# A routing that chooses on logits, gates that are a softmax over two, and slots read from the banks

## The reference

```python
logits = jnp.einsum('bsd,de->bse', x, gate_w) + gate_b
probs = jax.nn.softmax(logits, axis=-1)
top_probs, top_idx = jax.lax.top_k(probs, 2)
top_probs = top_probs / jnp.sum(top_probs, axis=-1, keepdims=True)
dispatch = jnp.sum(jax.nn.one_hot(top_idx, n_experts, dtype=x.dtype) * top_probs[..., None], axis=-2)
h1 = jnp.einsum('bsd,edh->bseh', x, w1)
h2 = jnp.einsum('bsd,edh->bseh', x, w2)
hidden = jax.nn.silu(h1) * h2
expert_out = jnp.einsum('bseh,eho->bseo', hidden, w3)
return jnp.einsum('bseo,bse->bso', expert_out, dispatch)
```

## Time and profile before

| | |
|---|---|
| median of 3 runs | 683.85 us (684.36, 678.06, 683.85) |
| the profiled execution | 683.36 us, span 681.3 us |
| mean granted clock of TensorE | 0.905 of 2.4 GHz |
| TensorE busy | 554.9 us, 81% |
| VectorE busy | 348.6 us, 51% |
| GpSimd busy | 408.2 us, 60% |
| ScalarE busy | 342.1 us, 50% |

### The profile page before, as it was taken

One profiled execution on the slowest core, in us unless ns is written; L12 is line 12 of the kernel. 1 busy time (PEld: TensorE's weight loads), 2 busy tenths in 40 slices (PEclk: granted clock), 3 DMA queues, 4 the chain that ended last, 5 costly groups with the idle time before them and its releaser, 6 DMA issues.

```text
span 681.3 us, 15719 instructions
## 1 busy us (share of the span) xinstructions
PE 554.9 (81%) x5422; PEld 468.6 (69%) x5423; DVE 348.6 (51%) x1021; ACT 342.1 (50%) x801; POOL 408.2 (60%) x468
## 2 busy tenths in 40 slices
PE   2477788778779999999999999959649729999960
PEld 2466667657547777677777678748639729999960
DVE  6977787846620171212001274784875405555563
ACT  4467668886547243674122552522515406666640
POOL 1568789767567388675333330037747777777771
PEclk9689999979869699999999988978978959999995
DMA  8452322212055455322219200001123123333457
GB/s 296 161 140 82 85 73 81 67 47 70 13 180 201 154 174 171 128 94 99 88 47 331 61 1 1 0 23 52 52 61 98 52 85 99 98 97 98 128 204 242
DMA packets 56288, 72.15 MB, mean 106 GB/s; under 512 B 9086, under 2 KB 46934, under 8 KB 55614
## 3 DMA queue, kind: packets, MB, share of 16 engines
q1 hardware_dynamic: 49374, 58.36, 27.5%
q0 software_dynamic: 5120, 10.57, 4.7%
q10 hardware_dynamic: 1728, 2.36, 0.9%
HBM read 55.83 MB, written 21.69 MB: 114 GB/s over the span
## 4 chain that ended last, share of the span: by engine, by line
PE 56%; DVE 14%; POOL 9%; issue 9%; ACT 7%; DMA 3%; SPq 1%; POOLq 0%; DVEq 0%; ACTq 0%
PE bank L836 12%; PE bank L798 9%; PE bank L781 8%; PE bank L902 7%; PE bank L847 6%; POOL gathered_or_att L580 3%; POOL padded_or_w L571 3%; ACT normed L947 2%; POOL gathered_or_att L589 2%; PE bank L325 2%; DVE ln_stats L1133 2%; PE bank L796 2%; PE bank L827 2%; PE bank L733 2%; PE bank L867 1%
## 5 line engine op out<-in xcount | busy, mean ns | idle before, releaser
L615 POOL TENSOR_TENSOR padded_or_w<-padded_or_w,gathered_or_att 128x384 f32<-128x384 f32 x96 | 95.4, 1000 | 80.7 <-ACT padded_or_w L1021 77.0
L632 POOL DMA_INDIRECT sorted_x<-normed,slot x72 | 71.2, 989 | 80.0 <-DVE slot L1395 51.4
L1021 ACT ACTIVATE padded_or_w<-bank,moe_b 128x384 f32<-128x384 f32 x96 | 55.3, 579 | 107.2 <-PE bank L781 107.1
L651 POOL DMA_INDIRECT returned<-gathered_or_att,home_of_slot x88 | 87.2, 991 | 26.8 <-issue 19.8
L798 PEld LDWEIGHTS bank<-moe_or_conv,padded_or_w 128*128 128x128 f32 x576 | 80.6, 197 | 30.9 <-issue 9.8
L798 PE MATMUL bank<-moe_or_conv,padded_or_w 128*128 128x128 f32 x576 | 83.9, 284 | 0.0
L781 PE MATMUL bank<-chan_major,moe_or_conv 128*128 128x384 f32 x192 | 82.7, 517 | 0.1
L671 PE MATMUL bank<-padded_or_w 64*64 64x64 f32 x1152 | 47.5, 233 | 27.3 <-issue 15.9
L1459 DVE TENSOR_TENSOR att_or_moe<-att_or_moe,bank 128x256 f32<-128x256 f32 x88 | 37.0, 420 | 61.2 <-ACT att_or_moe L1035 39.9
L671 PEld LDWEIGHTS bank<-padded_or_w 64*64 64x64 f32 x1152 | 41.5, 145 | 36.6 <-issue 32.8
L580 POOL TENSOR_TENSOR gathered_or_att<-gathered_or_att,score_max 128x384 f32<-128x384 f32 x48 | 39.9, 830 | 34.5 <-DVE score_max L1217 33.7
(11 more groups left out here) (214 smaller groups left out, 1122.8 us busy)
## 6 DMA issues: line engine op xcount, KB each, us to landing
gathered_or_att<-combine SPq DMA_DIRECT2D x24, 768.0 KB, 4.2
padded_or_w<-windows SPq DMA_DIRECT2D x192, 48.0 KB, 2.0
sorted_x<-in_pad_rows SPq DMA_DIRECT2D x22, 260.0 KB, 7.1
padded_or_w<-sorted_x SPq DMA_DIRECT2D x22, 260.0 KB
padded_or_w<-in_moe_w SPq DMA_DIRECT2D x8, 512.0 KB, 5.4
qy<-returned SPq DMA_DIRECT2D x6, 384.0 KB, 5.8
out<-residual ACTq DMA_DIRECT2D x12, 192.0 KB, 2.1
normed<-returned SPq DMA_DIRECT2D x6, 384.0 KB, 5.4
```

The costliest lines, as they stand in the source:

```text
L615: nc.gpsimd.tensor_tensor(HB[n % DRING], HB[n % DRING], GB_[k % 3][:, n % 4, :], ALU.mult).then_inc(S("gated"), 1)
L632: nc.gpsimd.indirect_dma_start(xs_dram, bass.IndirectOffsetOnAxis(ap=POS[b][:, k, t:t + 1], axis=0), TNR[b][:, t, :], None).then_inc(S(don ...
L651: nc.gpsimd.indirect_dma_start(yt_dram, bass.IndirectOffsetOnAxis(ap=HOMES[b][:, j:j + 1], axis=0), YR[k * RING + j % RING], None).then_in ...
L1021: nc.scalar.activation(HB[n % DRING], banks[HBANK[n % 2]][:, 0:DG], ACT.Gelu, bias=B1C[:, e:e + 1]).then_inc(S("gelu"), 1)
```

## The change

The second routing (16 experts) takes its two experts by the largest logits instead of the largest probabilities, so that shift, exponential, sum and division fall away ahead of the choice. The gate is made of the two chosen logits: e = exp(second - first), first gate 1 / (1 + e), second e / (1 + e). VectorE signals the difference (`logit_gap`) right after the second maximum, ScalarE answers with an exponential of 18 values a partition (`gap_exp`). In the list, `RE` moves to the middle of ScalarE's six normalization groups, and `RC` piece 0 behind them; VectorE has no part in those groups, so its own order is the same. A chosen logit is taken out by adding -1e38 where a probability was by adding -2.

In the slots, the matrix of ones meets the mask read in expert order, so that the counts lie in bank 7 as the scan wants them, and the scan reads the bank. The 0/1 factors that restart the scan at each expert (SAME) and the matrix TRO = TRI - ONE are built once, in `centre_gate`. As TRO's product subtracts the tokens from this one to its tile's end, the sum that includes the tile can be used as it is, and the subtraction of the tile's count goes. The two products change places.

```diff
@@ -175,6 +175,9 @@
         LGP = [sb(f"logits_of_norm{b}", [P, TT * EX[1]]) for b in range(NB)]
+        GEXP = sb("gate_exp", [P, TT])
+        SAME = sb("same_expert", [P, EX[1] * TT])
+        TRO = sb("not_before", [P, P])
         GST = sb("gn_stats", [P, 6, 6])
...
@@ -807,8 +810,8 @@
                 pe.wait_ge(S("chosen"), b + 1)
-                nc.tensor.matmul(banks[6][:, 0:TT * E], TRI, RT[:, 5, 0:TT * E], start=True, stop=True)
-                nc.tensor.matmul(banks[7][:, 0:TT * E], ONE, RT[:, 5, 0:TT * E], start=True, stop=True).then_inc(S("prefix"), 1)
+                nc.tensor.matmul(banks[7][:, 0:TT * E], ONE, RT[:, 5, 0:TT * E].rearrange("p (t e) -> p e t", e=E), start=True, stop=True)
+                nc.tensor.matmul(banks[6][:, 0:TT * E], TRO[:, :], RT[:, 5, 0:TT * E], start=True, stop=True).then_inc(S("prefix"), 1)
@@ -1008,9 +1011,10 @@
                     t_wait_read(act, group_no[("LG", l, b)])
+                    nc.scalar.activation(RT[:, 1, 0:TT * EX[l]], RT[:, 0, 0:TT * EX[l]], ACT.Exp).then_inc(S("logit_exp"), 1)
                 else:
-                    act.wait_ge(S("logit_shift"), b + 1)
-                nc.scalar.activation(RT[:, 1, 0:TT * EX[l]], RT[:, 0, 0:TT * EX[l]], ACT.Exp).then_inc(S("logit_exp"), 1)
+                    act.wait_ge(S("logit_gap"), b + 1)
+                    nc.scalar.activation(GEXP[:, :], RV[:, 3, :], ACT.Exp).then_inc(S("gap_exp"), 1)
@@ -1260,8 +1264,6 @@
                         link(tt(row(0), row(0), over_t(GB[:, :]), ALU.add))
-                        link(nc.vector.tensor_reduce(v[0], row(0), AX, ALU.max))
-                        tt(row(0), row(0), over_e(v[0]), ALU.subtract).then_inc(S("logit_shift"), 1)
                         return
@@ -1269,7 +1271,7 @@
-                if piece == 1:
+                if piece == 1 and l == 0:
                     dve.wait_ge(S("logit_exp"), n + 1)
@@ -1277,19 +1279,24 @@
                     k = piece - 2
-                    link(nc.vector.tensor_reduce(v[k], row(1), AX, ALU.max))
-                    link(tt(row(0), row(1), over_e(v[k]), ALU.is_equal))
-                    link(tt(row(0), row(0), over_t(REV[:, 0:E]), ALU.mult))
-                    link(nc.vector.tensor_reduce(v[2], row(0), AX, ALU.max))
-                    link(tt(row(2 + k), row(0), over_e(v[2]), ALU.is_equal))
+                    a, same, out_of = (row(1), row(0), -2.0) if l == 0 else (row(0), row(1), -1e38)
+                    link(nc.vector.tensor_reduce(v[k], a, AX, ALU.max))
+                    if l and k:
+                        tt(v[3], v[1], v[0], ALU.subtract).then_inc(S("logit_gap"), 1)
+                    link(tt(same, a, over_e(v[k]), ALU.is_equal))
+                    link(tt(same, same, over_t(REV[:, 0:E]), ALU.mult))
+                    link(nc.vector.tensor_reduce(v[2], same, AX, ALU.max))
+                    link(tt(row(2 + k), same, over_e(v[2]), ALU.is_equal))
                     if k == 0:
-                        link(nc.vector.scalar_tensor_tensor(row(1), row(2), -2.0, row(1), ALU.mult, ALU.add))
+                        link(nc.vector.scalar_tensor_tensor(a, row(2), out_of, a, ALU.mult, ALU.add))
...
                         tt(row(5), row(2), row(3), ALU.add).then_inc(S("chosen"), 1)
-                    link(tt(v[2], v[0], v[1], ALU.add))
-                    if l == 0:
+                        dve.wait_ge(S("gap_exp"), b + 1)
+                        link(ts(v[2], GEXP[:, :], 1.0, None, ALU.add))
+                    else:
+                        link(tt(v[2], v[0], v[1], ALU.add))
                         link(nc.vector.tensor_scalar_max(v[2], v[2], 1e-12))
@@ -1297,8 +1304,8 @@
                         dve.wait_ge(S("homes_set"), 2 * NB)
-                        tt(TNR[b][:, :, P + 1], v[0], v[3], ALU.mult)
-                        tt(NEXT[b][:, :, 1], v[1], v[3], ALU.mult).then_inc(S("first_gates"), 1)
+                        nc.vector.tensor_copy(TNR[b][:, :, P + 1], v[3])
+                        tt(NEXT[b][:, :, 1], GEXP[:, :], v[3], ALU.mult).then_inc(S("first_gates"), 1)
@@ -1308,6 +1315,9 @@
                 m = group_no[("GC", k)]
+                link(nc.vector.memset(SAME[:, :], 1.0))
+                link(nc.vector.memset(SAME[:, :].rearrange("p (e t) -> p e t", t=TT)[:, :, 0:1], 0.0))
+                link(tt(TRO[:, :], TRI, ONE, ALU.subtract))
                 t_wait_full(dve, m)
@@ -1353,19 +1363,12 @@
                 dve.wait_ge(S("prefix"), b + 1)
-                tot = RT[:, 0, 0:c].rearrange("p (e t) -> p e t", t=TT)
-                one = RT[:, 1, 0:c].rearrange("p (e t) -> p e t", t=TT)
-                nc.vector.memset(RT[:, 1, 0:c], 1.0).then_inc(S("dve_chain"), 1)
-                chain[0] += 1
-                link(nc.vector.tensor_copy(tot, banks[7][:, 0:c].rearrange("p (t e) -> p e t", e=E)))
-                link(nc.vector.memset(one[:, :, 0:1], 0.0))
-                link(nc.vector.tensor_tensor_scan(RT[:, 4, 0:c], RT[:, 1, 0:c], RT[:, 0, 0:c], 0.0, ALU.mult, ALU.add))
+                link(nc.vector.tensor_tensor_scan(RT[:, 4, 0:c], SAME[:, :], banks[7][:, 0:c], 0.0, ALU.mult, ALU.add))
                 run_ = RT[:, 4, 0:c].rearrange("p (e t) -> p e t", t=TT)
...
                 tmp = RT[:, 1, 0:c].rearrange("p (e t) -> p e t", t=TT)
-                nc.vector.tensor_copy(cnt, run_[:, :, TT - 1])
-                link(tt(tot, run_, tot, ALU.subtract))
+                link(nc.vector.tensor_copy(cnt, run_[:, :, TT - 1]))
@@ -1384,10 +1387,10 @@
-                link(tt(row(4), tot.rearrange("p e t -> p t e"), banks[6][:, 0:c].rearrange("p (t e) -> p t e", e=E), ALU.add))
-                link(tt(row(1), row(4), over_t(room), ALU.is_ge))
+                link(tt(row(0), run_.rearrange("p e t -> p t e"), banks[6][:, 0:c].rearrange("p (t e) -> p t e", e=E), ALU.add))
+                link(tt(row(1), row(0), over_t(room), ALU.is_ge))
                 link(tt(row(1), row(1), over_t(delta), ALU.mult))
-                link(tt(row(4), row(4), over_t(base), ALU.add))
+                link(tt(row(4), row(0), over_t(base), ALU.add))
                 link(tt(row(4), row(4), row(1), ALU.add))
...
                     link(tt(row(0), row(2 + k), row(4), ALU.mult))
```

More of the change, by code:

```diff
@@ L248, in metaformer_program @@
                   *taps(1, 0, 9), *[(kind, 0, g) for g in range(NG) for kind in ("XZ", "LZ")], *groups("AN", "XL", 1), *taps(1, 9, 15),
-                  *normed("LR", 1, 0)[:3], ("RC", 1, 0, 0), ("RE", 1, 0), *groups("LT", "LR", 1, 0), *choice(1, 0, 1, 6), *taps(1, 15, 42), ("RP", 0), *taps(1, 42, 54),
+                  *normed("LR", 1, 0)[:3], *groups("LT", "LR", 1, 0)[:3], ("RE", 1, 0), *groups("LT", "LR", 1, 0)[3:], ("RC", 1, 0, 0), *choice(1, 0, 1, 6), *taps(1, 15, 42), ("RP", 0), *taps(1, 42, 54),
                   ("RS", 0), ("GN", "XM", 1), ("KW", 6, "hc_ready", 2 * NB), ("GS", "XM", 1), ("GQ", "XM", 1), ("XMH", 1), ("RJ", 0),
                   *[("XU", 1, n) for n in range(8)], ("GN", "XU", 1), ("KW", 30, "up_out", 8 * NB), ("GS", "XU", 1), ("GQ", "XU", 1), ("KW", 10, "up_out", 8 * NB), *groups("XUH", 1), *[(kind, 1, g) for g in range(NG) for kind in ("XZ", "LZ")],
-                  *normed("LR", 1, 1)[:3], ("RC", 1, 1, 0), ("RE", 1, 1), *groups("LT", "LR", 1, 1), ("KW", 34, "up_out", 8 * NB), *choice(1, 1, 1, 6), ("RP", 1), ("KW", 16, "up_out", 8 * NB), ("RS", 1), ("RJ", 1),
+                  *normed("LR", 1, 1)[:3], *groups("LT", "LR", 1, 1)[:3], ("RE", 1, 1), *groups("LT", "LR", 1, 1)[3:], ("RC", 1, 1, 0), ("KW", 34, "up_out", 8 * NB), *choice(1, 1, 1, 6), ("RP", 1), ("KW", 16, "up_out", 8 * NB), ("RS", 1), ("RJ", 1),
                   *[("M", b) for b in range(NB)], *[("F", b) for b in range(NB)]]
```

## The result

| | before | changed |
|---|---|---|
| median | 684.01 us (20 runs, 678.06 to 689.9) | 680.28 us (20 runs, 673.05 to 686.64) |
| ratio | | 0.993, 95% interval 0.9901 to 0.9958 |
| profiled execution | 683.36 us, span 681.3 | 681.42 us, span 679.4 |

Some executions of either kernel run at a lower granted clock and take over 1.5% longer than its fastest; the ratio leaves them out, the medians don't. The change is worth 0.7%, 4.8 us, with an interval of 2.9 to 6.8 us. That interval holds the forecast gain of 6.24 us as well, so the time alone can't say which of the prediction's terms came true; the traces can.

A forecast was written before the change was run, and what follows sets the result against it. The path was taken to run through VectorE's routing chain in image 1, and its slots in both images, to the scatter. 2.57 + 2.36 + 1.31 = 6.24 us gain, forecast 677.5 us, range 672.5 to 681.5.

The forecast's parts named there:

- rival A: Image 1's products: TensorE's clock has fallen when the mask comes; gain 4.93 us, 678.9 by the median; chance 0.20.
- B: Ones product's stepped mask read costs 0.5 us in each image; gain 5.24, or 3.9 with rival A; chance 0.10.
- Part 5: Matrix-of-ones product reading the mask in steps of 16 values: taken at 0, upper bound 0.5 us an image.
- Part 7: Image 1's two products: TensorE's clock taken as still high, a gain of 1.31 us; lower bound 0.
- Part 1: No softmax ahead of the second routing's choice: gain 2.57 us in image 1; image 0's 2.6 gained and lost again.
- Part 2: Gates from an 18-element exponential after nine of ScalarE's normalizations: covered, two us of slack, put at nothing.
- Parts 3 and 4: Slots from the banks: gain 1.18 us an image; scan reading a bank: 0, bounds 0 to 0.19 an image.
- Part 6: Two fills and a subtraction built once ahead of VectorE's gate centring: nothing, 0.7 us without the idle time there.
- C: Clock stays high under image 1's second convolution and first fillers: 3.2 us more, 674.4; chance 0.10.
- D: Image 0's 1.18 us from the slots are lost because something other than VectorE is late there: 678.8; chance 0.06.
- E: Scatter or send-back follows a pace of its own, so nothing arrives: 683.9; chance 0.05.
- F: Stepped mask read many times dearer than doubled, a loss from 2.5 us an image; chance 0.04.

The follow-up runs named there:

- kernel 1: The kernel before with only the choice on logits, the gates and the exponential's place changed: 679.78 us, ratio 0.9979 to the kernel before.
- kernel 6: The changed kernel with ScalarE's small exponential ahead of all its normalizations: 686.15 us in one run.
- kernel 3: The changed kernel with VectorE writing the mask in expert order, so both products read it without steps: 678.8 us, ratio 0.994 to the kernel before.
- Kernel 5: The changed kernel with 46 filler pairs in place of 34 ahead of image 1's products: 678.79 us, ratio 0.9938 to the kernel before.
- kernel 9: Mask in expert order, 46 filler pairs, image 0's early products, plus 16 filler pairs for 30 behind the second convolution, on the changed kernel: 673.2 us, ratio 0.9891.
- kernels 1 and 2: The second is the kernel before with only the scan from the bank, stepped product and what is built once: 682.51 us, ratio 0.9978.

## Why the prediction was right, and where it was not

The forecast was a gain of 6.24 us, to 677.5; the gain is 4.8 by the ratio and 4.6 by the marks, and the median 680.28. The direction, the place and the mechanism hold; what was shown is rival A with half of B, not the forecast itself. The measured time lies in the range because the range had been drawn to take in A with B; two of the forecast's terms, parts 5 and 7, failed, and one of its own signs of being wrong came: image 0's first product is much longer than the second.

- **Part 1**, 2.57 us in image 1: 2.62 measured, 2.67 alone. That image 0's share is gained and lost again: shown by VectorE's wait of 5.99 us and by kernel 1, where logits 0 to group norm stays at 23.42.
- **Part 2**, covered: two us of slack foreseen, 2.0 measured (490.71 to 492.71), and kernel 6 shows that even a worse place is covered.
- **Parts 3 and 4**, 1.18 us an image and a free read of the bank: the scan took 754 ns from the bank and 757 before. Image 1 gained 1.22. Image 0 gained 0.76, and 1.26 when the product is plain (kernel 3).
- **Part 5** failed. I took the stepped read at 0 because L887, with runs of four values, cost nothing. It was the upper bound: 0.97 in place of 0.48 us. The rule of the Trainium skill ("SBUF — State Buffer", section "Door 1: The DMA port swizzle") gave the right sign where my nearest row didn't apply; runs of four are its free case and single values its dear one, and I had written that down and still gone by the row. It is worth one image and not two, as image 1's products ran at 1.2 GHz, where the step costs nothing. The rule alone doesn't say that, and rival B with A had counted both images (3.9 us; 4.4 with one).
- **Part 6**, covered: shown, though 1.2 us rather than 0.7.
- **Part 7** failed: 1.31 us for the clock, and none of it came. The mask came after an idle stretch of 3.50 us, as foreseen, but the clock was at 0.50 from then on. I had leaned on the row of 5.1 us at 1.00, which had one small product in the middle. This stretch had none, and neither had the one of before in which the clock fell. Kernel 5 shows the mechanism and its size: with the clock kept the products give 0.6 us, as the stepped read takes the rest back, and 1.04 with a plain read (product to scan 2.32 against 1.28). So the term was also too large, 1.31 against 1.04 measured with both: for image 0 I had taken the first product's start from the chain of waits (439.55), and the timeline has 439.38, so 0.17 of it was never there.
- **The rivals** C and D: not seen in the changed kernel (clock 0.51 from 455 to 468; image 0's gain arrived). E was excluded by GpSimd's idle time, rightly at this size: the 7.39 us shrank to 3.28, and kernel 9 shows the other side of that bound. F was far off: a doubling and not a dozen.

The sum as it should have been, with parts 1, 3 in image 0 (0.76 + 0.49), 3 in image 1 and 5: 2.62 + 1.25 + 1.22 - 0.49 = 4.6 us.

## What to carry to other kernels

A saving ahead of a queue that isn't there yet is only a longer wait: when a chain between engines is shortened, look at what stands ahead of the next engine's part, and move that part up, here by one number, for 2.7 us more; ask too how much of that the old kernel could have had. A layout change can move a part of its cost elsewhere: the reordering copy went, the matmul paid half a us for it in one image, and writing the mask in order paid 0.2. When timed runs spread over 1.7% and the gain is 0.7%, cut the traces at events common to both kernels; the distances of kernels 1 and 2 gave the changed kernel's sum to 0.1 us (4.67 against 4.60).

## What was unexpected of the hardware

- A product of 288 fp32 columns whose moving operand is read in steps of 16 values takes 0.97 us at 2.4 GHz against 0.48 read plainly, and at 1.2 GHz 1.33 against 1.32. Here the step costs only what the high clock would have gained.
- VectorE took as much longer for a transposed output as for a transposed operand: 652 against 457 ns for 288 elements, as 636 against 446.
- Ahead of image 1's products TensorE's clock stayed at 1.00 for 3.2 us of idle time in the kernel before and 3.4 in the changed one, and was at 0.50 from there; in the changed kernel that was just as the work came.
- A 128 x 128 subtraction on VectorE took 746 ns beside the dense mixture, more than a 128 x 288 addition in the routing (457). It began while GpSimd was in an addition that ran from 253.54 to 254.53 us, and ended 0.16 us behind it; it lies so in five other traces too. That it waited for GpSimd is not shown.
